# Where the sums over keys stand in TensorE's step of a pipelined attention stage

## The chip, the core and the metric

The kernel runs on one core of a Trainium2 chip. The metric is the device time of one execution in microseconds (us), as the median of several executions. The engines of the core have these names in what follows: TensorE (PE in the profile; PEld for its weight loads), VectorE (DVE), ScalarE (ACT), GpSimd (POOL) and SyncE (SP). Each runs its own list of instructions in order, and they wait for one another on semaphores.

## The reference

A two-layer decoder on 64 sequences of 128 tokens with 128 features: per layer an attention, a cross-attention and a mixture of experts, each followed by a residual sum and a layer norm. The change touches the first of these six blocks alone, an attention with a second-order Taylor expansion in place of the softmax:

```python
normed = rms_norm(x, gamma)
q = (normed @ w_q).reshape(b, n, h, dh).transpose(0, 2, 1, 3)          # h = 8 heads, dh = 16
kv = (normed @ w_kv).reshape(b, n, 2, h, dh).transpose(2, 0, 3, 1, 4)
k, v = (kv[0], kv[1])
q = second_taylor_expansion(q * dh ** (-0.5))     # [1, x, x (x) x / sqrt 2]
k = second_taylor_expansion(k)
kv_state = jnp.einsum('bhnd,bhne->bhde', k, v)
k_sum = jnp.sum(k, axis=2)
den = jnp.einsum('bhnd,bhd->bhn', q, k_sum)
out = jnp.einsum('bhnd,bhde->bhne', q, kv_state) / jnp.maximum(den, EPS)[..., None]
out = out.transpose(0, 2, 1, 3).reshape(b, n, h * dh) @ w_out
x = _layernorm(x + out)
```

The inner product of two expanded vectors is 1 + s + s*s/2 with s = q.k, so the kernel never builds the expansion: it squares a shifted score (the "weights"), multiplies these by v with a column of ones beside it, and sums over the keys.

## The kernel before

`taylor_attention` is the first stage. It goes through the 64 sequences as a software pipeline with eight stages: `each_step` calls `step(a, b, f, c, p, h, u, n)` on every engine for t = 0 to 70, and the eight names are the sequences t, t-1, ... t-7 (None outside 0 to 63). So one step of the loop works on eight sequences, and each engine's instructions of a step stand in the order in which its own `step` lists them.

TensorE's step has these parts, in this order:

1. T: the transposes of the normed tokens of sequence f (L339) and of the attention output of u (L341).
2. S: the scores of sequence c, four matmuls on strips of 32 rows (L350). They wait for `q_done`, `k_done` and `weights_done` of what VectorE and ScalarE did in the step before.
3. B: the two transposes back of the sums of sequence h (L357). They wait for `sums_done` to reach h + 1 (L352), that is for VectorE's copy of these sums out of PSUM in the step before.
4. q of f (L364), the output projection y of u (L366), in every second step the sums of v (L372), then k and v of f (L375, L376).
5. U: the sums over keys of sequence p, eight matmuls on strips of 32 columns (L386), into `sums_bank`. They wait for `v_done`, for `weights_done` of p, and for `sums_done` to reach p, since `sums_bank` is single and VectorE must have emptied it of the sequence before. As h is p - 1, this is the very count for which B of the same step waits.

VectorE's step: the scaled tokens `xs` of b (L276, behind GpSimd's `inv_norm`), then for h the denominator `den` (L281, behind B's `back_ps`), its reciprocal (L283) and the output `o` (L287), then `q_masked` of f (L296), the residual `z` of u (L301) with its statistics (L303, L306), the copy `sums` of p (L313, two instructions, behind U's `sums_ps`), and the normed output X of n (L319).

ScalarE's step: `xsT` and `oT` out of PSUM (L227, L230), the weights of c (L235, behind S), then k, in every second step `v_sum`, v of f (L239 to L245), and the squares of a (L253). GpSimd's step is four small instructions, among them `inv_norm` (L195), behind the squares. A barrier of all engines stands between the first stage and the second.

Of the kernel before, what the change touches and what calls it, by code (L numbers as in the profile page):

```python
# [22 lines left out]
P = 128  # L23
# [85 lines left out]
def taylor_attention(chip, n_seq, X, opening, x_loaded, later_loads, blank, fills, w, consts):  # L109
# [6 lines left out]
    with ExitStack() as ctx:  # L116
        def sb(name, shape):
            return chip.sb(ctx, "taylor_" + name, shape)

        def sem(name):  # L120
            return chip.sem("taylor_" + name)
# [16 lines left out]
        v_strip = sb("v_strip", [P, 4, H, 32])  # L138
        weights = sb("weights", [P, 2, 4, 2, P])
# [11 lines left out]
        kv_bank, sums_bank, back_bank = (chip.banks[:, n, 0:2 * P] for n in (1, 2, 3))  # L151
# [6 lines left out]
        q_ps, kv_ps, q_done, k_done, v_done, s_ps, weights_done = (  # L158
            sem(n) for n in ("q_ps", "kv_ps", "q_done", "k_done", "v_done", "s_ps", "weights_done"))
        v_sum_ps, v_sum_done = sem("v_sum_ps"), sem("v_sum_done")  # L160
        sums_ps, sums_done, back_ps, den_done, inv_den_done, o_done, y_ps = (
            sem(n) for n in ("sums_ps", "sums_done", "back_ps", "den_done", "inv_den_done", "o_done", "y_ps"))
# [5 lines left out]
        def each_step(step):  # L168
            for t in range(n_seq + STAGES - 1):
                step(*[t - s if 0 <= t - s < n_seq else None for s in range(STAGES)])  # L170
# [153 lines left out]
        @block.tensor  # L324
        def _(pe):
            ident = consts["ident"]
            pe.wait_ge(ready, 9)

            def step(a, b, f, c, p, h, u, n):
                if f is not None:  # L330
                    pe.wait_ge(xs_done, f + 1)
                    if f >= 1:
                        pe.wait_ge(q_done, f)
                if u is not None:
                    pe.wait_ge(o_done, u + 1)
                    if u >= 1:
                        pe.wait_ge(z_done, u)
                if f is not None:
                    pe.transpose(xsT_bank, xs[:, f % 2], ident).then_inc(xsT_ps, 1)  # L339
                if u is not None:  # L340
                    pe.transpose(oT_bank, o[:, u % 2], ident).then_inc(oT_ps, 1)  # L341
                if c is not None:
                    s = c % 2
                    pe.wait_ge(q_done, c + 1)
                    pe.wait_ge(k_done, c + 1)
                    if c >= 1:
                        pe.wait_ge(weights_done, c)
                    for g in range(4):
                        strip = slice(32 * g, 32 * g + 32)
                        last = pe.matmul(s_banks[:, g], kT[strip, s], q_masked[strip, s], start=True, stop=True)  # L350
                    last.then_inc(s_ps, 1)
                if h is not None:  # L352
                    pe.wait_ge(sums_done, h + 1)
                    if h >= 1:
                        pe.wait_ge(o_done, h)
                    for m in range(2):
                        last = pe.transpose(back_bank[:, m * P:(m + 1) * P], sums[:, h % 2, m], ident)  # L357
                    last.then_inc(back_ps, 1)
                if f is not None:
                    pe.wait_ge(xsT_done, f + 1)  # L360
                if u is not None:
                    pe.wait_ge(oT_done, u + 1)
                if f is not None:
                    pe.matmul(q_bank, wq[:], xsT[:, f % 2], start=True, stop=True).then_inc(q_ps, 1)  # L364
                if u is not None:
                    pe.matmul(y_bank, oT[:, u % 2], w["wo"], start=True, stop=True).then_inc(y_ps, 1)  # L366
                if f is not None:
                    if f >= 1:
                        pe.wait_ge(v_done, f)
                    if f % 2 == 1:  # L370
                        for m in range(2):
                            last = pe.matmul(v_sum_bank[:, m], wv_strip[:, 4 * m:4 * m + 4].rearrange("p h d -> p (h d)"),  # L372
                                             x_sum[:, (f - 1) % 4:(f - 1) % 4 + 2], start=True, stop=True)
                        last.then_inc(v_sum_ps, 1)
                    pe.matmul(kv_bank[:, 0:P], wk[:], xsT[:, f % 2], start=True, stop=True)  # L375
                    pe.matmul(kv_bank[:, P:2 * P], xsT[:, f % 2], wv[:], start=True, stop=True).then_inc(kv_ps, 1)  # L376
                if p is not None:
                    pe.wait_ge(v_done, p + 1)
                    if p >= 1:
                        pe.wait_ge(sums_done, p)  # L380
                    pe.wait_ge(weights_done, p + 1)
                    for m in range(2):
                        part = slice(m * P, (m + 1) * P)
                        for i in range(4):
                            head = 4 * m + i
                            last = pe.matmul(sums_bank[32 * i:32 * i + 32, part], v_strip[:, p % 4, head],  # L386
                                             weights[:, p % 2, head // 2, head % 2], start=True, stop=True)
                    last.then_inc(sums_ps, 1)

            each_step(step)  # L390


# [1894 lines left out]
```

## Time and profile before

| What | us |
|---|---|
| three executions | 2766.38, 2772.31, 4171.66 |
| their median | 2772.31 |
| the profiled execution, its own time | 2773.75 |
| its span, from first to last instruction | 2772.0 |
| end of the first stage in it, about | 228 |

The profile is of one execution. Times in its rows are in us from the start of the span. A busy TensorE is not TensorE at its peak: matmuls overlap, and where one row ends is modelled, so distances between the starts of rows say more than their lengths. A row of the timeline merges instructions of one kind that follow each other, with their count behind the x. What stands in square brackets at a row's end is the idle time of the engine before it and what ended that.

### The profile page before, as it was taken

What the parts mean: (1) busy time and instruction counts of PE and PEld (TensorE: products, weight loads), DVE (VectorE), ACT (ScalarE), POOL (GpSimd) and SP (SyncE); (2) the same over time, 40 slices, a digit from 0 to 9 for tenths busy, and PEclk for the clock granted to TensorE, in tenths of its full rate; (3) what the DMA queues carried; (4) which work ended last, traced back from release to release, by engine and by line L of the source; (5) the groups of instructions that cost most, each with busy time, mean ns of one, the idle gap of its engine ahead of it and who ended that gap; (6) DMA issues with size and microseconds to landing.
All of it is one profiled execution on the core that took longest, in us unless ns stands there. A gap on an engine that the chain in (4) does not pass through costs nothing. (4 is left out here: it accounts for less than half of the span.)

```text
span 2772.0 us, 61590 instructions
## 1 busy us (share of the span) xinstructions
PE 2534.0 (91%) x19168; PEld 1864.5 (67%) x19168; DVE 1904.9 (69%) x5298; ACT 1671.0 (60%) x4543; POOL 1694.9 (61%) x2110
## 2 busy tenths in 40 slices
PE   8998999999999289996999999969999999699996
PEld 6665887877877289993555555547766666458993
DVE  6884677787777355555777777765788886445655
ACT  6773666666665234444766666639888887623334
POOL 3442334555555645554888888846688887724675
PEclk9998999999999699998999999979999999899998
DMA  8932467777774122214100000000011010011336
GB/s 260 338 107 68 151 215 226 234 224 224 223 220 129 54 65 71 72 58 129 58 11 9 9 11 9 7 25 13 16 30 30 30 30 17 30 30 54 93 93 194
DMA packets 274799, 267.86 MB, mean 97 GB/s; under 512 B 30060, under 2 KB 253561, under 8 KB 274096
## 3 DMA queue, kind: packets, MB, share of 16 engines
q1 hardware_dynamic: 256912, 228.42, 27.2%
q0 software_dynamic: 17280, 34.13, 3.6%
q8 instruction: 161, 2.64, 0.4%
q10 hardware_dynamic: 288, 1.38, 0.2%
q14 instruction: 158, 1.29, 0.1%
HBM read 101.24 MB, written 151.85 MB: 91 GB/s over the span
## 5 line engine op out<-in xcount | busy, mean ns | idle before, releaser
L779 POOL TENSOR_TENSOR wide_probs<-wide_exps,wide_inv_sum 128x616 f32<-128x616 f32 x128 | 168.3, 1315 | 305.6 <-DVE wide_inv_sum L1580 293.0
L749 POOL TENSOR_TENSOR causal_exps<-causal_biased,causal_neg_max 128x512 f32<-128x512 f32 x256 | 262.8, 1036 | 76.4 <-DVE causal_neg_max L1594 76.2
L758 POOL DMA_INDIRECT sorted_x<-send,place_i x240 | 244.1, 1017 | 84.2 <-ACT send L1233 44.0
L1289 ACT ACTIVATE rotary_exps<-banks,rotary_neg_max 128x77 f32<-128x77 f32 x1024 | 248.7, 341 | 19.3 <-DVE rotary_neg_max L1594 19.1
L1764 POOL DMA_INDIRECT results<-gelu_tile_out,gelu_dest_i x142 | 140.1, 986 | 142.2 <-DVE gelu_tile_out L1920 120.0
L1539 DVE TENSOR_TENSOR causal_biased<-banks,regions 128x512 f32<-128x512 f32 x256 | 163.6, 680 | 80.7 <-PE banks L1115 80.4
L1764 POOL DMA_INDIRECT results<-swiglu_tile_out,swiglu_dest_i x142 | 144.6, 1019 | 116.7 <-DVE swiglu_tile_out L1915 59.4
L1833 ACT ACTIVATE gelu_hidden<-banks,gelu_slot 128x256 f32<-128x256 f32 x284 | 116.6, 470 | 159.5 <-PE banks L2010 159.4
L1258 ACT ACTIVATE causal_exps<-causal_exps 128x512 f32<-128x512 f32 x256 | 161.2, 630 | 71.4 <-POOL causal_exps L749 71.4
L1594 DVE TENSOR_REDUCE rotary_neg_max<-banks 128x4 f32<-128x308 f32 x256 | 121.7, 475 | 113.5 <-PE banks L1129 105.1
L1273 ACT ACTIVATE causal_probsT<-banks 128x512 f32<-128x512 f32 x256 | 151.6, 592 | 79.3 <-PE banks L1140 79.3
L1140 PEld LDWEIGHTS banks<-first,causal_exps 128*128 128x128 f32 x1024 | 107.2, 141 | 135.6 <-ACT causal_exps L1258 93.1
L1129 PE MATMUL banks<-rotary_keys,rotary_qT 128*128 128x308 f32 x512 | 192.1, 458 | 4.5 <-ACT rotary_exps L1289 4.1
L1091 PE MATMUL banks<-wide_folded,wide_probsT 128*128 128x128 f32 x1280 | 187.7, 278 | 6.8 <-DVE wide_z L1524 3.4
L703 POOL TENSOR_TENSOR rotary_keys<-rotary_kT,rest 128x308 f32<-128x308 f32 x256 | 176.6, 706 | 22.8 <-ACT rotary_kT L894 19.9
L1129 PE MATMUL banks<-wide_keys,wide_xT 128*128 128x308 f32 x512 | 180.7, 434 | 2.4 <-DVE wide_exps L1601 2.2
L1140 PE MATMUL banks<-first,causal_exps 128*128 128x128 f32 x1024 | 167.8, 286 | 12.2 <-ACT causal_exps L1258 12.2
L1273 ACT ACTIVATE rotary_probsT<-banks 77x512 f32<-77x512 f32 x256 | 155.1, 606 | 37.8 <-PE banks L1140 37.2
L1091 PEld LDWEIGHTS banks<-wide_folded,wide_probsT 128*128 128x128 f32 x1280 | 169.1, 194 | 8.1 <-issue 4.5
L1594 DVE TENSOR_REDUCE causal_neg_max<-causal_biased 128x4 f32<-128x512 f32 x256 | 168.0, 677 | 2.7 <-POOL causal_exps L749 2.1
L915 PE MATMUL banks<-regions,wide_v_context 128*128 128x512 f32 (+1 forms) x312 | 163.8, 607 | 5.0 <-ACT wide_staged L1183 3.3
L835 PE MATMUL banks<-wide_ctxT,regions 128*128 128x154 f32 x1024 | 166.5, 296 | 0.7 <-ACT wide_keys L869 0.6
(385 smaller groups left out, 7018.3 us busy)
## 6 DMA issues: line engine op xcount, KB each, us to landing
v_dram<-wide_staged SPq DMA_DIRECT2D x38, 1024.0 KB, 4.4
sorted_x<-blank SPq DMA_DIRECT2D x1, 34848.0 KB, 116.8
sorted_x<-blank SPq DMA_DIRECT2D x24, 1452.0 KB, 8.7
wide_folded<-v_dram SPq DMA_DIRECT2D x128, 256.0 KB
gelu_tile_in<-sorted_x SPq DMA_DIRECT2D x71, 132.0 KB, 2.1
swiglu_tile_in<-sorted_x SPq DMA_DIRECT2D x71, 132.0 KB, 2.1
gelu_back<-results SPq DMA_DIRECT2D x16, 512.0 KB, 8.0
swiglu_back<-results SPq DMA_DIRECT2D x16, 512.0 KB, 5.4
```

What stands on the lines that cost most here:

```text
L703: engine.tensor_tensor(keys[:, b, heads], kT[:, pair.c % 2, b, 0:NK].unsqueeze(1).to_broadcast([P, HU, NK]), mask[:, heads].unsqueeze(2).t ...
L749: pool.tensor_tensor(exps[:, (NU * pair.c + m) % ES], biased[:, m % BS].rearrange("p (h n) -> p h n", h=HU), neg_max[:, m % SLOTS].unsquee ...
L758: pool.indirect_dma_start(route["sorted_x"], bass.IndirectOffsetOnAxis(ap=r_place_i[:, b % 2, which, n // 2:n // 2 + 1], axis=0), send[:, ...
L779: pool.tensor_tensor(probs[:, half % SLOTS, 0:HH * NK].rearrange("p (k h) -> p h k", h=HH), exps[:, half % EB], inv_sum[:, half % SLOTS].u ...
L835: last = pe.matmul(f_bank[:, n * 2 * NK:(n + 1) * 2 * NK], product[:, first + n], ctxT[:, s4], start=True, stop=True)
L1091: last = pe.matmul(o_bank[0][:, b * P:(b + 1) * P], probsT[:, half % 2, n * P:(n + 1) * P], folded[:, pair.c % SPARE, b, g, n], start=g == ...
L1129: pe.matmul(s_bank[k % 2][:, 0:HU * NK], q, moving, start=True, stop=True).then_inc(s_ps, 1)
L1140: last = pe.transpose(p_bank[n % 2][0:NK, h * P:(h + 1) * P], exps[:, (NU * pair.c + n) % ES, h], ident)
L1273: act.activation(probsT[0:NK, n % 2], p_bank[n % 2][0:NK], ACT.Copy).then_inc(probsT_done, 1)
L1289: last = act.activation(exps[:, (NU * c.c + k) % ES, h], scores[:, h * NK:(h + 1) * NK], ACT.Exp, bias=neg_max[:, k % SLOTS, h:h + 1])
L1594: dve.tensor_reduce(neg_max[:, k % SLOTS], scores.rearrange("p (h n) -> p h n", h=HU), AX.X, ALU.max, negate=True).then_inc(max_done, 1)
L1764: pool.indirect_dma_start(results, bass.IndirectOffsetOnAxis(ap=dest_i[:, t % YR, j:j + 1], axis=0), tile_out[:, t % YR, j], None, bounds_ ...
```

## The change

In TensorE's step of the first stage, part U stands between T and S instead of at the end of the step. The instructions, their semaphores and their operands are the same; so the order T, S, B, q, y, k, v, U becomes T, U, S, B, q, y, k, v. No other engine's list changes.

```diff
                 if u is not None:
                     pe.transpose(oT_bank, o[:, u % 2], ident).then_inc(oT_ps, 1)
+                if p is not None:
+                    pe.wait_ge(v_done, p + 1)
+                    if p >= 1:
+                        pe.wait_ge(sums_done, p)
+                    pe.wait_ge(weights_done, p + 1)
+                    for m in range(2):
+                        part = slice(m * P, (m + 1) * P)
+                        for i in range(4):
+                            head = 4 * m + i
+                            last = pe.matmul(sums_bank[32 * i:32 * i + 32, part], v_strip[:, p % 4, head],
+                                             weights[:, p % 2, head // 2, head % 2], start=True, stop=True)
+                    last.then_inc(sums_ps, 1)
                 if c is not None:
                     s = c % 2
                     pe.wait_ge(q_done, c + 1)
...
                     pe.matmul(kv_bank[:, 0:P], wk[:], xsT[:, f % 2], start=True, stop=True)
                     pe.matmul(kv_bank[:, P:2 * P], xsT[:, f % 2], wv[:], start=True, stop=True).then_inc(kv_ps, 1)
-                if p is not None:
-                    pe.wait_ge(v_done, p + 1)
...
-                    last.then_inc(sums_ps, 1)
 
             each_step(step)
```

## Rows read from the trace of the kernel before

**Rows 1.** Windows: length, busy us per engine (instructions), granted clock, DMA share, GB/s
```profile
20.93:217.40 196.47, 190.58 (x2319) 137.46 (x2317) 163.68 (x664) 143.75 (x514) 90.41 (x238) 1.00 0.71 219
```
**Rows 2.** Timeline of TensorE, one step and a half in the middle of the stage
```profile
99.39 0.65 PE L386 MATMUL banks<-taylor_weights,taylor_v_strip 128*32 128x128 f32 x16
99.97 0.33 PE L339 MATMUL banks<-first,taylor_xs 128*128 128x128 f32 x1
...
100.34 0.71 PE L350 MATMUL banks<-taylor_q_masked,taylor_kT 32*128 32x256 f32 x8
100.98 0.44 PE L357 MATMUL banks<-first,taylor_sums 128*128 128x128 f32 x2
...
103.05 0.30 PE L339 MATMUL banks<-first,taylor_xs 128*128 128x128 f32 x1 [0.16 <-DVE taylor_z L301]
...
103.39 0.71 PE L350 MATMUL banks<-taylor_q_masked,taylor_kT 32*128 32x256 f32 x8
104.14 0.44 PE L357 MATMUL banks<-first,taylor_sums 128*128 128x128 f32 x2
```
**Rows 3.** Timeline of VectorE in the same steps
```profile
100.11 0.61 DVE L313 TENSOR_SCALAR taylor_sums<-banks,taylor_v_sum 128x128 f32<-128x128 f32 x2
...
101.45 0.28 DVE L276 TENSOR_SCALAR taylor_xs<-X,taylor_inv_norm 128x128 f32<-128x128 f32 x1 [0.48 <-POOL taylor_inv_norm L195]
101.65 0.16 DVE L281 TENSOR_SCALAR taylor_den<-banks 128x8 f32<-128x8 f32 x1
...
103.34 0.18 DVE L306 BATCH_NORM_AGGREGATE taylor_mean_var<-taylor_stats 128x2 f32<-128x6 f32 x1
103.47 0.61 DVE L313 TENSOR_SCALAR taylor_sums<-banks,taylor_v_sum 128x128 f32<-128x128 f32 x2
...
104.61 0.17 DVE L281 TENSOR_SCALAR taylor_den<-banks 128x8 f32<-128x8 f32 x1
...
106.30 0.18 DVE L306 BATCH_NORM_AGGREGATE taylor_mean_var<-taylor_stats 128x2 f32<-128x6 f32 x1
106.55 0.62 DVE L313 TENSOR_SCALAR taylor_sums<-banks,taylor_v_sum 128x128 f32<-128x128 f32 x2
```
**Rows 4.** Timeline of ScalarE in the same step
```profile
101.12 1.02 ACT L235 ACTIVATE taylor_weights<-banks 128x1024 f32<-128x1024 f32 x1
...
102.88 0.20 ACT L253 ACTIVATION_READ_ACCUMULATOR taylor_squares<-X 128x1 f32 x1
```
**Rows 5.** Timeline of VectorE at the end of the stage, where its list is shorter
```profile
217.40 0.17 DVE L281 TENSOR_SCALAR taylor_den<-banks 128x8 f32<-128x8 f32 x1 [0.38 <-PE banks L357]
...
220.03 0.17 DVE L281 TENSOR_SCALAR taylor_den<-banks 128x8 f32<-128x8 f32 x1 [0.28 <-PE banks L357]
```
**Rows 6.** Groups of weight loads, first stage: busy us, mean ns, idle before
```profile
L350 PEld LDWEIGHTS banks<-taylor_q_masked,taylor_kT 32*128 32x128 f32 x512 | 20.7, 189 | 11.5 <-issue 11.4
```
**Rows 7.** Timeline of TensorE in the stage's first steps
```profile
15.31 1.24 PE L350 MATMUL banks<-taylor_q_masked,taylor_kT 32*128 32x256 f32 x8 [0.20 <-issue]
16.47 0.80 PE L364 MATMUL banks<-taylor_xsT,taylor_wq 128*128 128x128 f32 x2
...
18.05 1.08 PE L386 MATMUL banks<-taylor_weights,taylor_v_strip 128*32 128x128 f32 x16
19.07 0.48 PE L339 MATMUL banks<-first,taylor_xs 128*128 128x128 f32 x1
```
**Rows 8.** Windows at the end of the first stage and in the second
```profile
217.40:220.03 2.63, 1.54 (x23) 0.98 (x21) 2.14 (x9) 0.96 (x2) 0.74 (x2) 1.00 0.01 3
220.03:222.91 2.88, 1.78 (x23) 1.24 (x21) 2.15 (x9) 0.28 (x1) 0.74 (x2) 0.77 0.00 0
...
896.00:910.00 14.00, 9.29 (x54) 6.76 (x53) 11.58 (x34) 4.67 (x11) 7.11 (x9) 1.00 0.05 15
```
**Rows 9.** Timeline of TensorE behind the first two of these windows
```profile
219.56 0.44 PE L357 MATMUL banks<-first,taylor_sums 128*128 128x128 f32 x2 [0.78 <-DVE taylor_sums L313]
...
222.19 0.69 PE L357 MATMUL banks<-first,taylor_sums 128*128 128x128 f32 x2 [0.78 <-DVE taylor_sums L313]
```

More of the change, by code:

```diff
@@ L376, in step @@
                     pe.matmul(kv_bank[:, P:2 * P], xsT[:, f % 2], wv[:], start=True, stop=True).then_inc(kv_ps, 1)
-                if p is not None:
-                    pe.wait_ge(v_done, p + 1)
[L379 to L387, printed above, removed]
-                    last.then_inc(sums_ps, 1)
             each_step(step)
```

## The prediction

> **What bounds the stage now.** I read the windows first. From the first `den` of VectorE to the one of step 66, that is over 61 steps, the stage takes 196.47 us, or 3.22 us a step; TensorE shows 190.58 us busy, VectorE 163.68 and ScalarE 143.75, at a granted clock of 1.00 [rows 1]. A TensorE that is 97% busy looks like the bound. But its rows are modelled to overlap, so I went on to the timelines to see who waits for whom.
>
> There it is a ring between two engines. VectorE's copy of the sums ends at 104.08; B, which waits for it, starts 0.06 later, at 104.14 [rows 2, 3]. The next `den` waits for B and starts 0.47 behind B's start, at 104.61 [rows 2, 3]; at the end of the stage this wait is named outright on both rows [rows 5]. From `den` VectorE runs through its list without rest to the end of its next copy. That takes 2.43 us (101.65 to 103.47 + 0.61) or 2.56 (104.61 to 106.55 + 0.62) [rows 3]. So every second step is copy, B, `den`, list, copy: 0.06 + 0.47 + 2.56 = 3.09 us. The other step is longer since `xs` comes late from GpSimd (0.48 us of idle) and `den` stands behind it [rows 3]; B ends before `xs` does there and has some 0.2 us to spare (101.42 against 101.65) [rows 2, 3]. Two steps together are 2 x 3.22 = 6.44 us; the copies of one kind stand as far apart (100.11 to 106.55) [rows 3].
>
> What the reader is to see: in this ring only B stands between one copy and the next `den`. S runs before the copy is done (103.39 against 104.08), and U runs late in the step while VectorE is at `o`, `z` and the statistics. Both lie beside the ring.
>
> **The change, part by part.** Nothing is added or removed: the same 16 matmul records of U and 8 of S are issued per step, no DMA moves, and the queues of SP and POOL are not passed. What changes is the queue on TensorE behind the wait for `sums_done`.
>
> (1) U now waits, ahead of S, for the copy of the step before. Behind it in the queue stand S and then B, and for B waits `den`. So after each copy the ring now runs U, S, B where it ran B.
>
> (2) The cost of U in this place: the nearest row is U followed by T, 99.39 to 99.97, 0.58 us [rows 2]. U followed by S does not occur; both change the shape in which TensorE is used. I take 0.58. From below: at a change of shape the weight loads stop, ahead of S by 11.5 us / 64 = 0.18 us a step [rows 6]. If such a stop fell away behind U, 0.40 would be left. From above: the full length of U's row, 0.65 [rows 2].
>
> (3) The cost of S: where B followed S directly and no copy held it, 100.34 to 100.98, 0.64 us; its full row plus the usual gap would be 0.74 [rows 2]. I take 0.64, which is also the lower end.
>
> (4) What U gives back: in every second step the copy started late behind U (106.30 to 106.55 between statistics and copy against 103.34 to 103.47, so 0.12) [rows 3]. U is now done long before, so every step has the shorter list, 2.43.
>
> (5) The new ring: 0.06 + 0.58 + 0.64 + 0.47 + 2.43 = 4.18 us a step. `xs`, late in every second step before, started 0.73 behind the end of the copy (100.72 to 101.45) [rows 3]; `den` now comes 1.75 behind it, so this lateness is covered.
>
> (6) Is anything else late next? The weights start 0.07 behind the end of S, at 0.06 + 0.58 + 0.71 + 0.07 = 1.42 from the copy's end; ScalarE needs from there to the end of the squares 1.96 us (101.12 to 103.08) [rows 4], so all of it is done by 3.4 (3.5 with `v_sum`) of 4.18. Weights end at 2.44, and the next U needs them at 4.18. T follows `den` by 1.40 (101.65 to 103.05), that is at 3.15, well before U. These are covered; should S come over 1.7 us later than I say, ScalarE would become the ring.
>
> (7) Sum: 61 steps at 4.18 - 3.22 = 0.96 give 58.5 us. The following step has no S: U alone, 0.58. The pipeline's filling has waits of its own; I take 0 there, between -1 and +1 us. Together 59 us. The second stage starts behind a barrier, so I let it pass the delay on. The profiled execution's own time is 2773.75, which gives 2833; the median of the runs is 1.4 below it, so 2831. By the bounds: with U at 0.40 the ring is 4.00, +48 us, 2820; with 0.65 and 0.74 it is 4.35, +70 us, 2842.
>
> TensorE's weight loads are weighed here once more. Rows: between two matmul groups of different shape the loads stop for 0.18 us, "issue" in the profile, in nearly every step [rows 6]. The Trainium skill, "TensorE: Matmul & The Clock Gate", Part 2, Step-by-step, says that TensorE pulls weight loads ahead of matmuls in flight where row groups do not conflict or the background buffer takes them; by that, S's loads would run under U, the ring would be 4.00 and the time 2820. The rows speak against it at a change of shape.
>
> **The rivals.**
> *The short change of shape*: the loads of S slide under U. Time 2820, as worked out above: inside 2%. Against it stands the stop before S in nearly each of 64 steps [rows 6].
>
> *The clock falls.* TensorE has had almost no rest in this stage. In the new ring it rests some 0.6 us between T and U, and up to 0.5 us between v and T. The clock fell to the lower of its two levels (1.2 GHz) at the end of the stage, after steps in which TensorE rested 0.78 us ahead of B and some more ahead of T (1.00, then 0.77 as a mean over the fall) [rows 8, 9]. It stayed at the upper level (2.4 GHz) over 14 us of the second stage in which TensorE was busy for 9.29 [rows 8]; the new ring keeps 3.1 of 4.18. At the lower level B costs 0.25 more (0.69 against 0.44) [rows 9]; U and S, when they were slow in the first steps, took 1.02 to the next start instead of 0.58, and 1.16 instead of 0.64 [rows 2, 7]. So 1.2 us for each ring at that level; with one ring in four, 15 times 1.2 = 18 us: 2849.
>
> *The delay is hidden.* Between copy and `den` VectorE has X and `xs` to do, and in every second step `xs` waits for GpSimd: `den` came 0.93 behind the copy there and 0.53 in the other step (100.72 to 101.65, 104.08 to 104.61) [rows 3]. If U and S together fitted into this cover (0.40 on B's path in one step of two, nothing in the other), only the 0.12 of (4) would be left as a gain in 31 steps: 2772.31 - 4 = 2769. It decides at U + S under 0.4 us; the rows give 1.22, and not under 1.04.
>
> **How the numbers follow.** Forecast, ring of about 4.18 at full clock: 0.62, with a range of its own of 2826 to 2842. Short change of shape: 0.15. Clock: 0.20. Hidden: 0.03. The range for 8 in 10 takes in both slower rivals: 2818 to 2850. A measurement here tells about 2% from no change; 2% is 2827.8, only 3 us under my number. Slower by over 2%: 0.52 of the forecast's 0.62 and all of the clock's 0.20, 0.72. Within 2%: the rest of the forecast, 0.10, the short change, 0.15, and 0.01 of the hidden case, 0.26. Faster: 0.02.
>
> **What would show it.** In the profile after: U starts about 0.06 behind the end of the copy in each step and its wait names the copy; S follows 0.58 and B 1.22 behind U's start; `den` starts 1.75 behind the copy's end, idle on B in every step, while the idle before `xs` and the 0.12 before the copy are gone; `den` to `den` is 4.18; TensorE's busy share falls and the clock stays 1.00. A step shorter than 4.1 means that (2) is too dear; rows of U over 0.8 us mean the clock. I am wrong as a whole if B still follows the copy within 0.6 us, or if the second stage gives the delay back.

## The result, and the profile after

| | us |
|---|---|
| before, median | 2773.64 |
| after, median | 2834.4 (2833.65 to 2837.62) |
| ratio after to before, 95% interval | 1.0235, 1.0216 to 1.0254 |
| profiled execution after, its own time (span) | 2833.8 (2832.0) |

By the ratio the change makes the kernel 2.35% slower; 2831 was forecast. (The median of before has moved by 1.3 us, since one more execution of it was timed.) The ratio is taken over the fast executions and leaves out the one of 4171.66 us, so it is not the quotient of the two medians, which lie 60.8 us (2.2%) apart.

First the view with which the prediction began: the windows, from the first `den` to the one of step 66, as in [rows 1]. The columns are the length, the busy time and instructions of PE, PEld, DVE, ACT and POOL, the granted clock, the DMA share and GB/s.

```profile
20.93:279.15 258.22, 193.99 (x2318) 139.17 (x2317) 167.83 (x665) 140.14 (x514) 89.33 (x238) 1.00 0.55 167
```

The same 61 steps take 258.22 us instead of 196.47, or 4.23 us a step instead of 3.22. TensorE and VectorE do the same work as before (193.99 and 167.83 us against 190.58 and 163.68), but TensorE is now busy for 75% of the time and not 97%. The time has gone into waiting, on both engines.

The timeline of TensorE after, in the middle of the stage (in this kernel U is L351, S is L362, B is L369, v is L388):

```profile
150.06 0.65 PE L351 MATMUL banks<-taylor_weights,taylor_v_strip 128*32 128x128 f32 x16 [0.72 <-ACT taylor_v_strip L245]
150.63 0.71 PE L362 MATMUL banks<-taylor_q_masked,taylor_kT 32*128 32x256 f32 x8
151.28 0.44 PE L369 MATMUL banks<-first,taylor_sums 128*128 128x128 f32 x2
...
152.22 0.39 PE L388 MATMUL banks<-taylor_wv,taylor_xsT 128*128 128x128 f32 x2
153.16 0.30 PE L339 MATMUL banks<-first,taylor_xs 128*128 128x128 f32 x1 [0.55 <-DVE taylor_z L301]
153.29 0.27 PE L341 MATMUL banks<-first,taylor_o 128*128 128x128 f32 x1
154.29 0.64 PE L351 MATMUL banks<-taylor_weights,taylor_v_strip 128*32 128x128 f32 x16 [0.72 <-issue]
154.86 0.71 PE L362 MATMUL banks<-taylor_q_masked,taylor_kT 32*128 32x256 f32 x8
155.51 0.44 PE L369 MATMUL banks<-first,taylor_sums 128*128 128x128 f32 x2
```

And VectorE in the same steps:

```profile
150.81 0.28 DVE L276 TENSOR_SCALAR taylor_xs<-X,taylor_inv_norm 128x128 f32<-128x128 f32 x1 [0.60 <-POOL taylor_inv_norm L195]
151.75 0.17 DVE L281 TENSOR_SCALAR taylor_den<-banks 128x8 f32<-128x8 f32 x1 [0.66 <-PE banks L369]
...
153.44 0.18 DVE L306 BATCH_NORM_AGGREGATE taylor_mean_var<-taylor_stats 128x2 f32<-128x6 f32 x1
153.58 0.61 DVE L313 TENSOR_SCALAR taylor_sums<-banks,taylor_v_sum 128x128 f32<-128x128 f32 x2
154.10 0.34 DVE L319 TENSOR_SCALAR X<-taylor_z,taylor_mean_var,taylor_rstd 128x128 f32<-128x128 f32 x1
154.51 0.29 DVE L276 TENSOR_SCALAR taylor_xs<-X,taylor_inv_norm 128x128 f32<-128x128 f32 x1
155.98 0.17 DVE L281 TENSOR_SCALAR taylor_den<-banks 128x8 f32<-128x8 f32 x1 [1.18 <-PE banks L369]
```

The reader sees the ring go round once. The copy ends at 153.58 + 0.61 = 154.19; U starts at 154.29, S at 154.86, B at 155.51, `den` at 155.98. Before, B followed the copy by 0.06 and `den` came 0.53 behind it, or 0.93 in the steps with a late `xs` [rows 2, 3]; now `den` comes 1.79 behind it in both. Every `den` now waits for B (0.66 and 1.18 us of idle here). The groups of waits in the first stage (who waited for what, us in total, times, longest) say it for the whole stage:

```profile
DVE taylor_den L281 <- PE banks L369: 59.0, 62, 1.5
...
PEld banks L351 <- ACT taylor_v_strip L245: 29.4, 31, 1.1
```

The first row has 59.0 us in 62 waits, where the kernel before had six such waits in the stage, the last four of them at its end, as on both rows of [rows 5]. The second row is a trap. It puts U's wait in 31 steps down to ScalarE's v, and so does the timeline at 150.06; for the next U it names no engine ("issue"). Three counts are waited for there: v, the weights and the copy. The ScalarE row of v that is named for the U at 150.06 had long ended, and so had the weights that the U at 154.29 needs:

```profile
149.18 0.28 ACT L245 ACTIVATE taylor_v_strip<-banks 128x128 f32<-128x128 f32 x1
...
151.41 1.02 ACT L235 ACTIVATE taylor_weights<-banks 128x1024 f32<-128x1024 f32 x1 [1.24 <-PE banks L362]
```

```profile
149.35 0.61 DVE L313 TENSOR_SCALAR taylor_sums<-banks,taylor_v_sum 128x128 f32<-128x128 f32 x2
```

ScalarE was done with v at 149.46, and with the v of another sequence; the copy was done at 149.96. The weights ended at 152.43, 1.86 us before their U. U's first matmul is 0.10 behind the copy, in this step as in the next, and 0.09 to 0.11 in every step of the stage. That U waits for the copy is so far a reading of times; the second and third experiment test it.

### The profile page after: what moved, and what is told of

It is laid out like the page before. It is cut to its first block and busy times, and to the rows that moved or that the text cites. A ratio compares the mean times of both kernels' runs of the same rounds, so it can differ in the third digit from the quotient of the medians.

```text
span 2832.0 us, 61590 instructions
## 1 busy us (share of the span) xinstructions
PE 2534.4 (89%) x19168; PEld 1864.2 (66%) x19168; DVE 1910.9 (67%) x5298; ACT 1667.0 (59%) x4543; POOL 1693.9 (60%) x2110
```

## The experiments

Theory: the ring copy, U, S, B, `den`, list, copy sets the step, since U waits for a copy that is made late in VectorE's step. Main rival: the order as such costs, because the scores come later and with them ScalarE's weights and k. The four kernels ran on one chip, beside its own runs of before with a median of 2769.95 us, 3.7 us under the one above; the expectations are to be read with that in mind. The ratios of the four are to these runs; again they are not the quotients of the medians. As a second measure that no later stage can disturb, the end of the first stage is given: the start of ScalarE's first instruction of the second stage in the trace, which is of one execution of each kernel, 228.26 before and 290.82 after:

```profile
290.82 0.20 ACT L1172 ACTIVATE tanh_gate<-rest 128x1 f32<-128x1 f32 x1 [3.45 <-PEq L116]
```

| kernel | median us | ratio (95%) | stage's end, us | against before, us |
|---|---|---|---|---|
| after the change | 2834.4 | 1.0235 (1.0216 to 1.0254) | 290.82 | +62.6 |
| U between S and B | 2798.71 | 1.0091 (1.0059 to 1.0123) | 252.22 | +24.0 |
| changed order, two banks | 2784.42 | 1.0048 (1.0033 to 1.0063) | 242.76 | +14.5 |
| changed order, copy first | 2783.08 | 1.004 (1.0025 to 1.0056) | 240.91 | +12.7 |
| old order, squares early | 2763.6 | 0.998 (0.9964 to 0.9996) | 223.23 | -5.0 |

### U between S and B

The diff is against the kernel after; U is moved as a whole.

```diff
                 if u is not None:
                     pe.transpose(oT_bank, o[:, u % 2], ident).then_inc(oT_ps, 1)
-                if p is not None:
-                    pe.wait_ge(v_done, p + 1)
...
-                    last.then_inc(sums_ps, 1)
                 if c is not None:
...
                     last.then_inc(s_ps, 1)
+                if p is not None:
+                    pe.wait_ge(v_done, p + 1)
...
+                    last.then_inc(sums_ps, 1)
                 if h is not None:
                     pe.wait_ge(sums_done, h + 1)
```

> U stands between S and B, so S runs before the copy of the sums is done, and U still waits for it. Theory (the ring copy, U, S, B, den, list sets the step): only U is left in the ring, 0.10 + 0.58 + 0.47 + 2.43 = 3.58 us a step against 3.22 before and 4.23 after the change, so 61 x 0.36 = 22 us over before: about 2796 us. Rival (what costs is that the scores, and with them ScalarE's weights and k, come late; the wait of U is hidden): S is back in its old place, so about 2774 us.

Measured: 2798.71 us, 1.0091 of before, so 25 us more (the medians lie 28.8 us apart); the stage ends 24.0 us later, where 22 were expected. The timelines of TensorE and VectorE:

```profile
152.33 0.71 PE L350 MATMUL banks<-taylor_q_masked,taylor_kT 32*128 32x256 f32 x8
153.12 0.64 PE L361 MATMUL banks<-taylor_weights,taylor_v_strip 128*32 128x128 f32 x16
153.69 0.44 PE L369 MATMUL banks<-first,taylor_sums 128*128 128x128 f32 x2
```

```profile
150.59 0.17 DVE L281 TENSOR_SCALAR taylor_den<-banks 128x8 f32<-128x8 f32 x1 [0.54 <-PE banks L369]
...
152.41 0.61 DVE L313 TENSOR_SCALAR taylor_sums<-banks,taylor_v_sum 128x128 f32<-128x128 f32 x2
...
154.17 0.17 DVE L281 TENSOR_SCALAR taylor_den<-banks 128x8 f32<-128x8 f32 x1
```

S runs again before the copy is done (152.33 against 153.02). U is alone behind it, 0.10 after its end, and a step takes 154.17 - 150.59 = 3.58 us, as the theory had it. The rival falls: the scores are back in their old place, and two fifths of the loss (24.0 of 62.6 us) are still there. The other three fifths are S, which left the ring: 62.6 - 24.0 = 38.6 us over 61 steps is 0.63 a step, and S stands 0.65 ahead of B in the profile after.

### The changed order, with two banks for the sums

```diff
+        sums_banks = (sums_bank, chip.banks[:, 3, 2 * P:4 * P])
...
-                    if p >= 1:
-                        pe.wait_ge(sums_done, p)
+                    if p >= 2:
+                        pe.wait_ge(sums_done, p - 1)
...
-                            last = pe.matmul(sums_bank[32 * i:32 * i + 32, part], v_strip[:, p % 4, head],
+                            last = pe.matmul(sums_banks[p % 2][32 * i:32 * i + 32, part], v_strip[:, p % 4, head],
```

VectorE's copy reads `sums_banks[p % 2]` in the same way.

> The changed order T, U, S, B, but with two banks for the sums, so that U waits for the copy of two steps before instead of the last. Theory: U and S no longer stand behind the copy; the ring is then den, list up to z, T, U, S, B, den: 1.41 + 0.34 + 0.58 + 0.65 + 0.47 = 3.45 us a step, 61 x 0.23 = 14 us over before: about 2788 us. Rival (the order itself costs, scores late): U still stands ahead of S, so nothing is regained: about 2834 us.

Measured: 2784.42 us, 1.0048 of before; the stage ends 14.5 us later and not 62.6. The order is the changed one, S is as late in the list as in the kernel after, and 48 of the 63 us are regained by taking away what U waited for. So it is the wait for the copy, and not the order on TensorE as such, nor ScalarE's v that the profile had named. The timeline of TensorE:

```profile
150.40 0.30 PE L340 MATMUL banks<-first,taylor_xs 128*128 128x128 f32 x1 [0.59 <-DVE taylor_z L302]
150.54 0.27 PE L342 MATMUL banks<-first,taylor_o 128*128 128x128 f32 x1
150.74 0.65 PE L352 MATMUL banks<-taylor_weights,taylor_v_strip 128*32 128x128 f32 x16
151.32 0.71 PE L363 MATMUL banks<-taylor_q_masked,taylor_kT 32*128 32x256 f32 x8
151.96 0.44 PE L370 MATMUL banks<-first,taylor_sums 128*128 128x128 f32 x2
```

U follows T by 0.20 with no rest between them. The way from T to B is now 151.96 - 150.40 = 1.56 us, and T waits for `z`. So a second ring is left: `den`, `z`, T, U, S, B, `den`, 3.45 us by the sum above. In the old order it is the same without U's 0.58, 2.87 us, and so under the 3.22 of the step before. With U in it, it is over them: 61 x 0.23 = 14.0 of the 14.5 us. This last account rests on the sum; no run took the second ring away.

### The changed order, with the copy first on VectorE

```diff
             def step(a, b, f, c, p, h, u, n):
+                if p is not None:
+                    dve.wait_ge(sums_ps, p + 1)
...
+                    last.then_inc(sums_done, 1)
                 if b is not None:
                     dve.wait_ge(inv_norm_done, b + 1)
...
-                if p is not None:
-                    dve.wait_ge(sums_ps, p + 1)
...
-                    last.then_inc(sums_done, 1)
```

> The changed order and one bank, but VectorE copies the sums at the head of its step, while TensorE is at S and B, instead of near its end. Theory: the copy for which the next U waits is done long before; the ring is the one of e2, 3.45 us a step: about 2788 us. Rival (the order itself costs): about 2834 us. Third way: the copy ahead of den only lengthens VectorE's list (0.53 us): about 2834 + 32 = 2866 us.

Measured: 2783.08 us, 1.004 of before; the stage ends 12.7 us later. Here the bank is single and U waits for the copy of the step before, as in the kernel after; only this copy is made earlier. The timeline of VectorE:

```profile
150.89 0.61 DVE L278 TENSOR_SCALAR taylor_sums<-banks,taylor_v_sum 128x128 f32<-128x128 f32 x2 [0.35 <-PE banks L351]
151.41 0.28 DVE L285 TENSOR_SCALAR taylor_xs<-X,taylor_inv_norm 128x128 f32<-128x128 f32 x1
151.87 0.17 DVE L290 TENSOR_SCALAR taylor_den<-banks 128x8 f32<-128x8 f32 x1 [0.18 <-PE banks L369]
...
155.16 0.29 DVE L285 TENSOR_SCALAR taylor_xs<-X,taylor_inv_norm 128x128 f32<-128x128 f32 x1 [0.23 <-POOL taylor_inv_norm L195]
155.36 0.16 DVE L290 TENSOR_SCALAR taylor_den<-banks 128x8 f32<-128x8 f32 x1
```

The copy now falls into the time in which TensorE is at S and B, and VectorE has 0.18 us to spare ahead of the first `den` even so. At the second `den` it is not the copy but `xs` that is late, since it waits 0.23 for GpSimd. The third way, in which the copy lengthens the list, falls. A step is 155.36 - 151.87 = 3.49 us, with the next one 3.43. Two different cures of the same wait come out within 2 us of each other, at the ring that was worked out for both.

### The old order, with ScalarE's squares early

```diff
             def step(a, b, f, c, p, h, u, n):
...
+                if a is not None:
+                    per_part = n_seq // len(x_loaded)
...
                 if f is not None:
                     act.wait_ge(kv_ps, f + 1)
...
-                if a is not None:
-                    per_part = n_seq // len(x_loaded)
...
```

> The old order of TensorE; ScalarE does the squares ahead of k instead of last in its step, so that GpSimd's inv_norm and VectorE's xs come earlier in every second step. Theory: there xs held den for 0.2 us only, since B is bound by S at about the same time; 31 x 0.2 = 6 us: about 2767 us. Rival (the 0.48 us of idle before xs are all lost time): 31 x 0.48 = 15 us: about 2759 us.

Measured: 2763.6 us against 2769.95, a ratio of 0.998 whose interval stays just under 1; the stage ends 5.0 us earlier. This is the test of how I read the longer of the two steps before, in which `xs` was late. The idle time before `xs` is gone, and `den` now waits for B:

```profile
105.53 0.28 DVE L276 TENSOR_SCALAR taylor_xs<-X,taylor_inv_norm 128x128 f32<-128x128 f32 x1
106.09 0.17 DVE L281 TENSOR_SCALAR taylor_den<-banks 128x8 f32<-128x8 f32 x1 [0.28 <-PE banks L357]
```

If all of the 5.0 us come from this, then of the 0.48 us of idle before `xs` [rows 3] 5.0 / 31 = 0.16 was lost time in each pair of steps; the rest B would have taken anyway. It is the one version here that is faster than before and after, by a fifth of a per cent, which is barely clear of the noise.

## Why the prediction was right

Point by point:

(1) The ring holds: U, S and B follow each copy, in this order, and the two cures show that the wait for the copy is what puts them there. One sign that I had named did not come: U's wait names the copy in two of the stage's steps only, both at its end; elsewhere the profile names v or "issue".

(2) and (3) U to S takes 154.86 - 154.29 = 0.57 us and S to B 0.65, against 0.58 and 0.64 forecast. The rival of the short change of shape, with 0.40 for U, is out: the weight loads stop ahead of S as before (11.5 us then [rows 6]; the loads of S are L362 here).

```profile
L362 PEld LDWEIGHTS banks<-taylor_q_masked,taylor_kT 32*128 32x128 f32 x512 | 20.5, 187 | 13.2 <-issue 13.2
```

By the rule that was weighed there (the Trainium skill, "TensorE: Matmul & The Clock Gate", Part 2, Step-by-step: TensorE pulls weight loads ahead of matmuls in flight where the row groups do not conflict or the background buffer takes them) the stop behind U should have gone, if one of its two conditions held here; 13.2 us / 64 = 0.21 a step says that it has not. No run here shows which condition was missing.

(4) The shorter list is there: 151.75 to 154.19 is 2.44 us, and the copy starts 0.13 or 0.14 behind the statistics in every step.

(5) The ring is 4.23 and not 4.18. The term that was mis-sized is the first one: U starts 0.10 behind the copy's end, where I had taken the 0.06 of B. It is 0.10 in the kernel with U between S and B too. And in every eighth step the copy's row is longer:

```profile
98.34 0.74 DVE L313 TENSOR_SCALAR taylor_sums<-banks,taylor_v_sum 128x128 f32<-128x128 f32 x2
```

This is 0.13 us more than usual, eight times in the stage; what makes it so was not tried. The stage ends 62.6 us later, 3.6 more than the 59 of the sum. Of this, 60 steps at 0.05 more are 3.0, and the eight longer copies 8 x 0.13 = 1.0. The following step, taken at 0.58, grew by 0.81 (282.59 - 279.15 = 3.44 against 2.63 [rows 8]), 0.2 more. Against these, the first of the 61 steps was still a step of the filling and took 3.37 us, 0.8 less than the ring. That makes 3.4.

(6) Nothing else became late: ScalarE's weights, k, v and squares are done before they are wanted. One detail was wrong without effect: I had said that the idle time before `xs` would go. It is still there in every second step, with 0.60 us in the one shown, but there `xs` is done 0.66 us before `den` can start.

(7) The second stage passed on the delay, as forecast, but not to the microsecond: from the stage's end to the end of the span it is 2541.2 us after and 2543.7 before. In the four experiments the same rest is 2544.5, 2537.5, 2545.0 and 2535.4 us, with no relation to the first stage's length, so these 2.5 us are not an effect that I could name.

The other rivals. *The clock* stayed at 1.00, its upper level, through the 61 steps, though TensorE rested 0.72 us ahead of U in each step shown and 0.55 ahead of T in one of them. It fell only in the stage's last steps, as it had before [rows 8]: 0.92 as a mean from 279.15 to 282.59, then 0.50. The price of that rival was weaker than it looked, too: U and S were slow in the stage's first steps, but the granted clock reads 1.00 there as well (14 to 20 us, before), so no row shows what they cost at the lower level. *The delay hidden* is out: 0.66 to 1.18 us of idle time stand before `den`.

My own number was 2831 and my sum on the profiled execution's own time 2833; that execution took 2833.8. That it came so close has some luck in it: the 3.6 us that the stage took more than the sum were met by 2.5 that the rest took less.

## What to carry to other kernels

Where an engine's list is moved, look at each wait that moves with it and ask when in the other engine's step its count comes: a wait that cost nothing at the end of the step, because the count had long come, put U and then S behind it on the longest ring when it stood ahead of them. What joins the ring is the sum of the start-to-start distances of all groups that now stand between the releaser and the waiter (U and S, 1.22 us), and not the length of the moved group alone. The step grows by less where the old one had other waits in it: here by 4.23 - 3.22 = 1.01 us, since a late `xs` had held up every second `den` already. When such an order is wanted all the same, a second buffer, or an earlier place for the instruction that frees the first, can take most of it back, as 48 and 50 of the 63 us here.

## What was not expected

A wait of TensorE for VectorE ended in the first matmul 0.10 us behind the end of the copy when the group began with weight loads of strips (U), and 0.06 behind it with a plain transpose (B [rows 2, 3]); what makes the difference was not tried. And in a wait on three semaphores the profile's named releaser, ScalarE's v, had ended half a microsecond before the true one.
